# The softmax denominator's copy and reciprocal move from VectorE to ScalarE, at the head of the next pass

## What is computed

```python
scores = jnp.einsum('bqhd,bkhd->bhqk', qf, kf) / math.sqrt(V_HD)
probs = jax.nn.softmax(scores.astype(jnp.float32), axis=-1).astype(qf.dtype)
out = jnp.einsum('bhqk,bkhd->bqhd', probs, v)

def _ternary_weight(w, group_size):          # group_size = 64
    wb = w.astype(jnp.bfloat16)
    wg = wb.reshape(-1, group_size)
    scale = jnp.clip(jnp.mean(jnp.abs(wg), axis=-1, keepdims=True), 1e-08, None)
    q = jnp.clip(jnp.round(wg / scale), -1.0, 1.0)
    qs = (q * scale).reshape(w.shape).astype(w.dtype)
    return w + jax.lax.stop_gradient(qs - w)
```

## Time and profile before

| | us |
|---|---|
| median of the two timed runs | 8394.14 |
| the two runs | 8337.16 and 8451.12 |
| the profiled execution | 8361.3 |
| its span on the slowest core (core 0) | 8359.8 |
| spans of the other seven cores | 8314.4 to 8353.4 |

### The profile page before, as it was taken

The page is one execution under the profiler, slowest core; times in us unless marked ns, Lnnn a source line. Parts: engine busy times, 40 slices in busy tenths (PEclk is TensorE's granted clock), DMA queues, the critical chain, the costliest instruction groups (busy, mean ns, idle before and its releaser), DMA issues.

```text
span 8359.8 us, 54516 instructions; the slowest of 8 cores (8314.4 to 8359.8 us)
## 1 busy us (share of the span) xinstructions
PE 4824.1 (58%) x17696; PEld 1714.7 (21%) x18032; DVE 2747.5 (33%) x2941; ACT 1297.4 (16%) x2018; POOL 1320.8 (16%) x2076
## 2 busy tenths in 40 slices
PE   2766665656654454554392266556765676557655
PEld 1321111111111111111141122222221222222221
DVE  3031666666655555555414311001100110011000
ACT  4233121211211111111014400000000000000000
POOL 0000101001023233233200011111111111111111
PEclk9888666666666666666695688998898889988898
DMA  4212222222221221221254433443344433443344
GB/s 103 43 53 55 65 59 58 63 57 62 59 55 45 50 53 45 51 54 44 45 96 156 135 76 88 166 163 83 80 149 158 110 77 123 165 135 77 96 161 151
DMA packets 470662, 745.46 MB, mean 89 GB/s; under 512 B 256210, under 2 KB 317811, under 8 KB 457587
## 3 DMA queue, kind: packets, MB, share of 16 engines
q0 software_dynamic: 210528, 557.22, 24.9%
q1 hardware_dynamic: 259860, 184.74, 7.4%
HBM read 690.68 MB, written 138.41 MB: 99 GB/s over the span
## 4 chain that ended last, share of the span: by engine, by line
PE 30%; DVE 24%; DMA 20%; issue 13%; POOL 6%; ACT 4%; SPq 2%; another core or an unknown queue 1%; DVEq 0%; ACTq 0%; POOLq 0%
PE pa L1227 13%; DMA pool<-w2t_scr 11%; PE pa L1305 6%; POOL w2t_scr L865 6%; DVE pool L822 3%; DVE pool L819 3%; DVE pool L801 3%; PE pa L1055 3%; DVE pool L904 3%; DMA pool<-wfc 2%; DMA pool<-wproj 2%; ACT pool L1233 2%; DVE pool L825 2%; PE pa L906 2%; DVE bigb L1237 1%
## 5 line engine op out<-in xcount | busy, mean ns | idle before, releaser
L1305 PE MATMUL pa<-pool,bigb 128*128 128x512 bf16 x4016 | 1020.7, 398 | 742.4 <-DMA pool<-w2t_scr 638.5
L1227 PE MATMUL pa<-biga,pool 128*128 128x512 bf16 x4008 | 1146.1, 450 | 58.5 <-DVE pool L1358 31.6
L997 ACT ACTIVATE pool<-pa 128x512 bf16<-128x512 f32 x1024 | 611.4, 597 | 2649.3 <-PE pa L994 2649.3
L906 PE MATMUL pa<-pool,cons 1*128 1x512 f32 x128 | 129.7, 1114 | 1110.8 <-DVE pool L904 1110.8
L865 POOL DMA_DIRECT2D w2t_scr<-pool x1024 | 544.0, 540 | 1243.6 <-DVE pool L852 1228.3
L1305 PEld LDWEIGHTS pa<-pool,bigb 128*128 128x128 bf16 x4096 | 382.6, 101 | 1378.8 <-issue 1045.1
L1237 DVE TENSOR_TENSOR bigb<-pool 128x512 bf16<-128x512 bf16 x256 | 108.9, 425 | 1505.7 <-ACT pool L1233 1505.7
L1333 DVE SCALAR_TENSOR_TENSOR pool<-pool 128x1024 bf16<-128x1024 bf16 x32 | 39.1, 1223 | 1701.8 <-ACT pool L1327 1701.8
L1227 PEld LDWEIGHTS pa<-biga,pool 128*128 128x128 bf16 x4096 | 439.0, 112 | 715.7 <-issue 432.3
L1214 POOL DMA_DIRECT2D pool<-w1t_scr x256 | 294.4, 1150 | 1808.2 <-PE pa L1227 1450.1
L801 DVE TENSOR_REDUCE pool<-pool 128x32 f32<-128x2048 bf16 x128 | 292.1, 2282 | 802.2 <-DMA pool<-wfc 428.9
(11 more groups left out here) (131 smaller groups left out, 4489.1 us busy)
## 6 DMA issues: line engine op xcount, KB each, us to landing
pool<-w2t_scr POOLq DMA_DIRECT2D x512, 512.0 KB, 3.5
pool<-w1t_scr POOLq DMA_DIRECT2D x256, 512.0 KB, 5.2
pool<-x SPq DMA_DIRECT2D x32, 1024.0 KB, 7.7
pool<-v_scr SPq DMA_DIRECT2D x128, 256.0 KB, 3.0
pool<-wfc POOLq DMA_DIRECT2D x64, 512.0 KB, 7.5
w1t_scr<-pool POOLq DMA_DIRECT2D x128, 256.0 KB, 2.9
pool<-wproj POOLq DMA_DIRECT2D x64, 512.0 KB, 6.7
w2t_scr<-pool POOLq DMA_DIRECT2D x1024, 32.0 KB, 1.8
```

The costliest lines, as they stand in the source:

```text
L906: e_bc = p.t(lambda e, kb_=kb: e.matmul(c.bank(kb_), c.sb_ones_row, rrow, start=True, stop=True, skip_group_check=True), after=[e_rc, c.e_ ...
L997: e_exp[kt] = p.s(lambda e, k_=kt, bs_=bs: e.activation(Ering[k_ % 3], c.bank(bs_), AF.Exp, scale=SM_SCALE), after=[e_s2, st.get(("ering", ...
L1227: e.matmul(c.bank(pb_), w1sb[b][:, d_ * 128:d_ * 128 + 128], c.xn3T[:, d_ * 2048 + ss * 512: d_ * 2048 + ss * 512 + 512], start=(d_ == 0), ...
L1305: t_=tt: e.matmul(c.pa[l_ * 2 + c2 // 2][:, (c2 % 2) * 512: (c2 % 2) * 512 + 512], h_sb[:, h_ * 512 + t_ * 128: h_ * 512 + t_ * 128 + 128] ...
```

## The change

`emit_tail` is cut in two. `tail_part1` runs at the head of the next pass, ahead of its loads and its attention loop: ScalarE copies the row of sums to `srow`, takes Ln of it into `rrow`, and exp(-x) of that back into `srow`, so that `srow` holds the reciprocal. `tail_part2` stands where `emit_tail` stood, behind the loop, and holds the broadcast matmul (which now reads `srow`), the copy of the bank, the product and the bias. The copy, the reciprocal and nothing else leave VectorE's list; ScalarE's gets three 1x512 operations ahead of the sixteen exponentials. The next row copy waits for the broadcast matmul, which reads `srow`, instead of for the reciprocal. For the last pass both parts stand behind it.

```diff
-    def emit_tail(item):
+    def tail_part1(item):
         h, qt, kb, ob, e_sum, e_pv = item
-        e_sr = p.v(lambda e, kb_=kb: e.tensor_copy(srow, c.bank(kb_)[0:1, :]),
+        e_sr = p.s(lambda e, kb_=kb: e.copy(srow, c.bank(kb_)[0:1, :]),
                    after=[e_sum, st.get("srow_user")])
         st[("bank", kb)] = e_sr
-        e_rc = p.v(lambda e: e.reciprocal(rrow, srow), after=[e_sr])
-        st["srow_user"] = e_rc
-        e_bc = p.t(lambda e, kb_=kb: e.matmul(c.bank(kb_), c.sb_ones_row, rrow,
+        e_ln = p.s(lambda e: e.activation(rrow, srow, AF.Ln), after=[e_sr])
+        e_rx = p.s(lambda e: e.activation(srow, rrow, AF.Exp, scale=-1.0),
+                   after=[e_ln])
+        return e_rx
+
+    def tail_part2(item, e_rx):
+        h, qt, kb, ob, e_sum, e_pv = item
+        e_bc = p.t(lambda e, kb_=kb: e.matmul(c.bank(kb_), c.sb_ones_row, srow,
                                               start=True, stop=True,
                                               skip_group_check=True),
-                   after=[e_rc, c.e_onesr])
+                   after=[e_rx, c.e_onesr])
+        st["srow_user"] = e_bc
         e_rbe = p.v(lambda e, kb_=kb: e.tensor_copy(rb, c.bank(kb_)),
                     after=[e_bc, st.get("rb_user")])
@@
     SB3 = (0, 1, 6)
+    pend_rx = [None]
     for qt in range(NQ):
         for h in range(NH):
@@
+            if pend_tail:
+                pend_rx[0] = tail_part1(pend_tail[0])
             e_qn = p.sydma(lambda e, q_=qt, h_=h, b=bi: e.dma_start(
@@
+            if pend_tail:
+                tail_part2(pend_tail.pop(0), pend_rx[0])
             pend_tail.append((h, qt, kb, ob, e_sum, e_pv))
-            if len(pend_tail) > 1:
-                emit_tail(pend_tail.pop(0))
@@
     while pend_tail:
-        emit_tail(pend_tail.pop(0))
+        e_rx = tail_part1(pend_tail[0])
+        tail_part2(pend_tail.pop(0), e_rx)
```

## The result

| | before | after |
|---|---|---|
| median, us (runs) | 8396.75 (10) | 7974.53 (11) |
| lowest and highest run, us | 8337.16, 8451.12 | 7959.03, 8053.22 |
| span of the profiled execution, us | 8359.8 | 7968.0 (core 4) |

The ratio is 0.9516, with a 95% interval from 0.9481 to 0.9551: the change saves 4.8%. The same kernel, timed again next to the first experiments, gave 0.9506 (0.948 to 0.9532), with medians of 8374.8 and 7953.3 us.

The account below looks back on a forecast made before the run. VectorE's list plus its errands was taken to bound attention. 63 x 6.41 = 404 us gained, less 2 in the second pass, gave 8361 - 402 = 7959 us, rounded to 7960; range 7915 to 8065.

Parts of the forecast that it names:

- The closed chain: In attention, VectorE's list plus the errands it orders from other engines sets the pace; first-half period 47.54 us.
- 6.41 us a pass, 404 in all: VectorE's tail loses row copy 0.77, reciprocal 3.35 and the 2.29 us wait for the broadcast matmul, 63 times.
- The broadcast matmul early, 9.4 us of cover: On TensorE it runs right behind the attention loop, ending about 2057.5 us; VectorE needs it only at about 2066.9.
- L849's first group early too: TensorE's first eight transposes behind the broadcast matmul also run early, their inputs done by about 2055 us; gain nothing.
- The stall changes its name: TensorE's wait moves from the old broadcast matmul to L849 waiting for L852, growing from 343 to about 1050 us.
- ScalarE at no cost: Copy, Ln and Exp at the head of a pass, about 2.2 us, fit in ScalarE's idle time, 23 us of cover.
- No table load in the stage: Ln and Exp alternating 64 times on ScalarE in attention need no new table load; L319's 1.283 us load stays single.
- The second pass, 2 us lost: There TensorE is late and the first exponential stands behind the three new operations, so this pass loses about 2 us.
- TensorE late: Rival: in the first half a clock staying at 0.50 makes L910 about 1.9 us late; 8018 us, chance 0.08.
- One half lost: Rival: in the second half spills or landings keep their own pace, losing 205 us; 8164 us, chance 0.03.
- No change: Rival: the broadcast matmul is hidden anyway in attention's loop, so the time stays 8361 us; chance 0.03.
- Slower: Rival: denser TensorE work in attention lowers the granted clock in feed-forward; about 8530 us, chance 0.02.

Follow-up runs that it names:

- the first experiments: Three edits of the changed kernel: row copy and reciprocal on VectorE under the landing, 7987.4 us; one more reciprocal, 8194.7 us; row work behind the loop, 7969.2 us.
- the third buffer: Third buffer of weights, each load issued one item ahead: 7384.8 us on the changed kernel, 7784.9 us on the kernel before.

## Why the prediction was right

Predicted 7960 us, from 7915 to 8065; measured 7974.5. The mechanism came as described. That the number is within 15 us is partly luck: the sum started from the profiled execution (8361 us), 36 us under the median that the kernel before turned out to have (8396.75), and the medians fell by 422 us, 20 more than the 402 forecast (421.5 when timed again). The stretch of attention explains 400 to 410 of these; the rest is within the scatter of the runs.

- *The closed chain.* Shown. Removing links (the change, the third buffer), adding one (the extra reciprocal) and moving one under a landing each moved the stretch of attention by about what the chain says, and 14 us of work off the chain didn't. The largest miss is the row put back on VectorE with three buffers, 232 us of 260.
- *6.41 us a pass, 404 in all.* The first half's period shown fell from 47.54 to 40.98 us, by 6.56, and the stage by 400 (402 forecast). The pass shown is a good one: the mean fell by 6.14 us in the first half and 6.55 in the second. Of the 6.41, 4.12 us a pass was VectorE's own work and 2.29 the errand. The busy time alone, 258 us, would have missed a third of the gain. In the first half the waits of L852 for its spills grew from 87.2 to 92.4 us and those for `wfc` from 236.2 to 238.2, which is most of the 9 us missing there.
- *The broadcast matmul early, 9.4 us of cover.* Measured 9.44 us in the pass shown.
- *L849's first group early too.* Right in the first half. In the second it waits for the first ternary item 29 times, 3.0 us in the mean, because the landing ends later there, and once for 25.2 us behind the last pass, where no loop stands ahead of it; 111.8 us in all. The forecast had taken the first half's pass for both. It cost nothing, since the group is needed only by the L852 behind the tail.
- *The stall changes its name.* Forecast about 1050 us of L849 waiting for L852, measured 1002.1, with 111.8 more for L825, which the forecast didn't have.
- *ScalarE at no cost.* The head of the pass:

```profile
2024.92 0.60 ACT L1006 ACTIVATE pool<-pa 128x512 bf16<-128x512 f32 x1 [0.56 <-PE pa L1003]
2027.86 0.57 ACT L901 COPY pool<-pa 1x512 f32<-1x512 f32 x1 [2.34 <-PE pa L911]
2028.52 0.63 ACT L904 ACTIVATE pool<-pool 1x512 f32<-1x512 f32 x1
2029.24 0.63 ACT L905 ACTIVATE pool<-pool 1x512 f32<-1x512 f32 x1
2046.31 0.60 ACT L1006 ACTIVATE pool<-pa 128x512 bf16<-128x512 f32 x1 [16.44 <-PE pa L1003]
```

The row copy starts behind the broadcast matmul of the pass before, the three end at 2029.87, and 16.44 us pass before the next exponential. The forecast's 23 us of cover were those of the old, longer pass; taking off the 6.4 that the pass gets shorter would have given nearly the right figure. The copy from PSUM, for which 0.63 us was taken, is 0.575:

```profile
L904 ACT ACTIVATE pool<-pool 1x512 f32<-1x512 f32 x64 | 40.2, 628 | 6.1 <-ACT pool L901 0.4
...
L901 ACT COPY pool<-pa 1x512 f32<-1x512 f32 x64 | 36.8, 575 | 148.1 <-PE pa L911 147.1 <-PE pa L967 1.0
...
L319 ACT ACT_TABLE_LOAD x1 | 1.3, 1283 | 1.2 <-DVE cons L317 1.2
```

- *No table load in the stage.* Shown: L319's single load is still the last; Ln and Exp alternate 64 times behind it. The Trainium skill's sentence that one set has both ("ScalarE: Activation LUTs", "Table sets: the hidden batching unit") agrees. What two switches a pass would cost no run here shows.
- *The second pass, 2 us lost.* The one place where the three stand ahead of an exponential that is due:

```profile
814.28 0.60 ACT L1006 ACTIVATE pool<-pa 128x512 bf16<-128x512 f32 x1 [0.57 <-PE pa L1003]
815.84 0.57 ACT L901 COPY pool<-pa 1x512 f32<-1x512 f32 x1 [0.96 <-PE pa L967]
...
818.04 1.52 ACT L1006 ACTIVATE pool<-pa 128x512 bf16<-128x512 f32 x3
...
836.99 0.69 DVE L916 COPY pool<-pa 128x512 f32<-128x512 f32 x1 [19.74 <-PE pa L911]
```

From the last exponential of the first loop to the copy of the bank it takes 836.99 - 814.28 = 22.7 us, and took 838.54 - 816.77 = 21.8 before (the earlier trace rows has the 838.54; 816.77 is the last exponential's start in the old trace, below). So about 1 us and not 2: part of the delay is made up, since TensorE has three tiles of scores ready and ScalarE takes them without a pause (three exponentials in 1.52 us).

```profile
816.77 0.60 ACT L997 ACTIVATE pool<-pa 128x512 bf16<-128x512 f32 x1 [0.57 <-PE pa L994]
```

- *The rivals.* TensorE late: not in the change, but from three buffers on, where the pass is 33 us. One half lost: no, the waits for landings and spills moved with the chain (for `w2t_scr` 262.4 us, and 261.1 before). No change: no. Slower, by a lower clock behind attention: no, it stayed 0.86, and is 0.86 with three buffers too, where attention is another 605 us shorter.

## What to carry to other kernels

Write out one period of the late engine's list in order of time and mark every errand that it sends to another engine and waits for. Each of its links has a price, its own length, and each idle stretch is a place where other work is free; the same reciprocal showed no cost under the landing, and 3.3 us a pass behind the ternary items. The largest wait in the list of waits (TensorE's 1110.8 us) was no price of anything; the landing, with 609.5, was worth 611 us of attention in this kernel and 605 in the changed one. When the chain gets shorter than another engine's round, that round takes over, as TensorE's begins to at 33 us a pass, and that of ScalarE and TensorE did with 48 operations more.

## What the runs showed of the hardware

The broadcast matmul (f32, 1x512, recorded as two) takes 2.04 us after a long idle time, as the forecast assumed, but 1.12 us right behind the loop, and the eight transposes behind it 0.62 us where they took 1.03 at its old place. TensorE had stood still for 15.79 us ahead of the first and not at all ahead of the second. The granted clock was 0.50 (1.2 GHz) from 2071.2 to 2074.4 us in the trace before and 1.00 (2.4 GHz) from 2026.6 to 2027.8 in the trace after. So these instructions, moved to the end of a busy stretch, got cheaper by the move itself. Here that went into the cover and not into the time.

On 1x512 in f32, VectorE's reciprocal is 3.34 us and ScalarE's Ln and Exp 0.63 us each.
